# Filler matmuls in seven gaps of each of the first three tails of a decoder kernel

## The chip, the core and the metric

One core of a Trainium2 chip runs the whole kernel. TensorE (PE, matmuls), VectorE (DVE), ScalarE (ACT) and GpSimd (POOL) each work through an instruction list of their own in order and meet only at semaphores; SyncE (SP) issues most loads. PSUM has eight banks of 128 x 512 f32; matmuls write there. The metric is the device time of one execution in microseconds (us), the median of three runs.

## The reference, cut to what matters

Four sequences of 512 tokens with 512 features pass through two layers of mixers, each followed by a layer norm:

```
x = layernorm(x + mamba_A(x))        # selective scan over 1024 channels, then a gated MLP of width 1408
x = layernorm(x + mamba_B(ctx, x))   # selective scan over 512 channels, gated by x
x = layernorm(x + moe(x))            # top 2 of 8 experts of width 352, and a shared MLP
x = layernorm(x + segment_attn(x))   # attention within groups of 4 and a learned memory
x = layernorm(x + cross(x, ctx))     # x times softmax(q k')
x = layernorm(x + bias_router(x))    # top 8 of 64 learned biases
selective scan:  h = exp(dt * A) * h + dt * B * u ;  y = sum_n C_n * h_n      (16 states n)
```

## The kernel before, in words

All arithmetic is f32. The work on one sequence has three parts.

**Heads** (tasks `c_*`, `p_*`) project and convolve the inputs of the two scans. Nearly all of them are done before the first tail begins.

**Units**: the scans. There are twelve units q, three for each sequence (one of 512 channels for mamba B, two of 512 channels for mamba A), each with 16 states n. A unit opens with four matmuls `dt_mm` (PE L899), each evacuated by two ACT instructions (L1321, L1322) before the next may start, since all go through bank 5. When the fourth is evacuated, ACT runs a chain of exp and log (`dt_exp`, `dt_b`, L1340 to L1351), and then DVE runs three products of 2048 elements (`dt_c`, L1603, L1608, L1614). A state then is a scan on DVE (`sa`, L1622), a product with B (L1535, from bank 5) and one with C (`sb`, L1630, from bank 7); PE broadcasts the rows of B and C into these banks (L787, L916), ACT makes exp(dt * A) into `da` (L1169), POOL adds up y (L1895). `fin` (L1636) closes a unit.

**Tails**: all else of a sequence b, one long chain of small dependent stages. In order: `mix` (output projection, L942, eight tasks, with `x1` L1649 on DVE), `t_sq` and `t_rs` (sum of squares on PE L950, its root on ACT, the scaling on DVE L1655), the gated MLP (`ffn_mm`/`ffn_mu` L969/L976, `ffn_ev` L1661/L1667, `ffn_down` L777), `res_t` (L1028), layer norm `ln 0` (DVE L1484 to L1491, ACT L1160 to L1421), `v_in` (L1043), `gate` (ACT L1430, DVE L1706/L1709, PE L1059), `ln 1`, its transposes `ln_t 1` (L1035) with an evacuation on ACT (L1426), routing, the shared MLP (`exp_*`), 15 expert blocks (`bx`, `bg`, `bt`, `bd`), a gather by POOL, `comb` (DVE L1687), `ln 2`, segment attention (`s_in`, `seg_*`, L1778), `ln 3`, cross attention (`xmix`, L1127), `ln 4`, and the biases (`bias_*`, PE L1134 to L1149).

Tail b of the first three sequences runs on PE while DVE scans the three units of sequence b + 1. `mix` of tail b + 1 needs the last `fin` of these units and the last `xmix` of tail b. So from there on what is left of the old tail (`ln 4` and the biases), the opening of a unit and the new `mix` are interleaved; I call this stretch a handover. The last tail has no scans beside it.

**What sets the order**: `plan()` lists every task and engine with a rank, a duration in us and what it comes after; `schedule()` simulates these and picks, on the engine that can start first, the task of the lowest rank that can start within `SLACK` of it. The order that comes out is written into each engine's instruction list. So a task that is added, or that must come after another, can change the order on all engines. On the chip nothing is picked: a task waits for its turn and its semaphores.

`KEEP` lists 14 places in the last tail: after a task, before a task, a count. There PE multiplies a constant matrix by a constant into bank 7, which no one reads. `plan()` gives such a task 0.43 us a matmul and makes the task named second wait for it.

## Time and profile before

| | |
|---|---|
| runs | 3093.26 us median (3091.72 to 3096.84) |
| profiled execution | 3097.64 us, span 3095.8 us |
| PE busy | 2570.3 us (83%) |
| DVE busy | 2407.2 us (78%) |
| ACT busy | 1242.9 us (40%) |
| POOL busy | 1053.6 us (34%) |
| granted TensorE clock, mean | 0.893 |
| matmuls into bank 7 from constants (L1039) | 100, in the last tail alone |

The clock is a share of full speed, which is 2.4 GHz; the rows show 1.00 and 0.50 (1.2 GHz), and values between them where a stretch holds both. The profile shows each f32 matmul as two instructions. A row of the timeline has the start, the time that its instructions span, the engine and line, what is written from what, the number of instructions, and in brackets how long the engine had been idle before and what ended that.

### The profile page before, as it was taken

To read this page: it belongs to the slowest core of one execution; us is meant where nothing else is said; L and a number is where in the kernel's file an instruction comes from. 1 tells how busy PE (TensorE), PEld (TensorE's weight loads), DVE (VectorE), ACT (ScalarE), POOL (GpSimd) and SP (SyncE) were. 2 spreads that over 40 slices of the span, in tenths; PEclk is the share of its full clock that TensorE was granted. 3 is DMA by queue.
4 is the path that set the end of the run, shared out by engine and by line. 5 is a ranking of instruction groups with operands and counts; after the bars stand their busy time and mean duration, and the time that the engine had idled before them with its cause. 6 is when DMAs were issued, how large, how long until landed. Compare 5 with 4: busy or idle time off the path is not lost.

```text
span 3095.8 us, 21549 instructions
## 1 busy us (share of the span) xinstructions
PE 2570.3 (83%) x6908; PEld 1236.9 (40%) x6908; DVE 2407.2 (78%) x1788; ACT 1242.9 (40%) x1993; POOL 1053.6 (34%) x299
## 2 busy tenths in 40 slices
PE   4787989888969887699798785898787859999996
PEld 1234434333434443344344443343444424455553
DVE  4996898998979988989899999798999984121122
ACT  4433456444253453453534534534445332021222
POOL 1333343344434446424434454245343441000000
PEclk6886999888989998789889997899898869999998
DMA  3124435323212674032126660221166502216920
GB/s 132 36 82 153 137 104 189 110 92 109 64 39 72 220 236 153 25 101 63 41 72 202 219 182 13 89 82 48 65 198 189 173 27 75 72 48 221 293 86 14
DMA packets 160392, 350.15 MB, mean 113 GB/s; under 512 B 30680, under 2 KB 48088, under 8 KB 155608
## 3 DMA queue, kind: packets, MB, share of 16 engines
q1 hardware_dynamic: 134680, 271.89, 28.5%
q10 hardware_dynamic: 20480, 60.10, 5.1%
q0 software_dynamic: 5120, 16.78, 1.6%
q8 instruction: 55, 0.90, 0.1%
q14 instruction: 57, 0.47, 0.0%
HBM read 304.55 MB, written 61.73 MB: 118 GB/s over the span
## 4 chain that ended last, share of the span: by engine, by line
PE 39%; DVE 33%; issue 12%; ACT 8%; POOL 4%; DMA 3%; ACTq 0%; DVEq 0%; SPq 0%; POOLq 0%
DVE hb L1622 14%; PE ps L969 6%; PE ps L976 6%; DVE hb L1630 4%; DVE hb L1535 4%; PE ps L777 3%; PE ps L824 3%; POOL ya L1895 3%; PE ps L831 2%; PE ps L942 2%; DMA ring<-in_w_edn 2%; PE ps L1012 2%; PE ps L1127 2%; PE ps L899 1%; ACT T L1421 1%
## 5 line engine op out<-in xcount | busy, mean ns | idle before, releaser
L1895 POOL TENSOR_TENSOR ya<-ya,hb 128x2048 f32<-128x2048 f32 x188 | 856.8, 4557 | 1327.9 <-DVE hb L1622 1245.1
L1622 DVE TENSOR_TENSOR_SCAN hb<-da,hb 128x2048 f32<-128x2048 f32 x192 | 855.9, 4458 | 2.0 <-ACT da L1169 0.7
L1169 ACT ACTIVATE da<-dl,pk 128x511 f32<-128x511 f32 x768 | 489.3, 711 | 403.6 <-DVE hb L1622 393.3
L1535 DVE TENSOR_TENSOR hb<-du,ps 128x2048 f32<-128x2048 f32 x192 | 435.8, 2270 | 35.2 <-POOL ya L1895 27.4
L1630 DVE TENSOR_TENSOR hb<-hb,ps 128x2048 f32<-128x2048 f32 x192 | 437.4, 2278 | 3.7 <-PE ps L916 2.9
L824 PE MATMUL ps<-V,ring 128*128 128x512 f32 x512 | 245.1, 632 | 23.4 <-DVE V L1563 11.5
L777 PE MATMUL ps<-ring,hid 128*128 128x512 f32 x544 | 246.8, 610 | 3.7 <-DVE hid L1667 3.7
L993 PE MATMUL ps<-ring,hid 128*128 128x352 f32 x480 | 199.1, 498 | 22.4 <-ACT hid L1392 16.7
L997 PE MATMUL ps<-ring,hid 128*128 128x352 f32 x480 | 194.0, 487 | 11.5 <-ACT X L1409 11.4
L1012 PE MATMUL ps<-ring,X 128*128 128x512 f32 x360 | 180.9, 638 | 15.7 <-DMA ring<-in_w_edn 15.0
L969 PE MATMUL ps<-T,ring 128*128 128x512 f32 x352 | 165.7, 615 | 14.9 <-DVE T L1655 14.9
L787 PE MATMUL ps<-bct,sel 64*128 64x512 f32 x192 | 100.8, 525 | 88.1 <-DVE hb L1535 78.2
L824 PEld LDWEIGHTS ps<-V,ring 128*128 128x128 f32 x512 | 101.9, 203 | 157.5 <-issue 142.5
L976 PE MATMUL ps<-T,ring 128*128 128x512 f32 x352 | 159.5, 596 | 0.0
L777 PEld LDWEIGHTS ps<-ring,hid 128*128 128x128 f32 x544 | 104.0, 194 | 135.9 <-issue 135.9
L916 PE MATMUL ps<-bct,sel 64*128 64x512 f32 x192 | 91.3, 476 | 78.9 <-DVE hb L1630 78.8
L1160 ACT ACT_TABLE_LOAD x44 | 56.5, 1283 | 231.8 <-DVE mv L1491 188.8
L787 PEld LDWEIGHTS ps<-bct,sel 64*128 64x128 f32 x192 | 37.1, 193 | 222.2 <-DVE hb L1535 108.4
L997 PEld LDWEIGHTS ps<-ring,hid 128*128 128x128 f32 x480 | 94.7, 203 | 74.1 <-ACT X L1409 24.3
L942 PE MATMUL ps<-yg,ring 128*128 128x512 f32 x256 | 122.6, 636 | 0.7 <-DVE yg L1636 0.7
L1672 DVE SCALAR_TENSOR_TENSOR T<-T,ps 128x352 f32<-128x352 f32 x60 | 30.5, 508 | 116.5 <-ACT T L1397 116.5
L993 PEld LDWEIGHTS ps<-ring,hid 128*128 128x128 f32 x480 | 88.4, 201 | 77.1 <-issue 40.3
(285 smaller groups left out, 3511.8 us busy)
## 6 DMA issues: line engine op xcount, KB each, us to landing
ring<-egu SPq DMA_DIRECT2D x240, 352.0 KB, 3.8
ring<-in_w_edn SPq DMA_DIRECT2D x72, 512.0 KB, 5.3
ring<-in_w_fgu SPq DMA_DIRECT2D x44, 512.0 KB, 3.6
hid<-xrows SPq DMA_DIRECT2D x60, 256.0 KB, 4.4
yrows<-X ACTq DMA_DIRECT2D x60, 256.0 KB, 4.4
ring<-wc SPq DMA_DIRECT2D x24, 512.0 KB, 4.2
ring<-in_w_egu SPq DMA_DIRECT2D x24, 512.0 KB, 3.5
ring<-in_w_edn SPq DMA_DIRECT2D x60, 192.0 KB, 4.0
```

What stands on the lines that cost most here:

```text
L777: i = pe.matmul(ps[:, e, :], hid[:, k - lo, e * P:(e + 1) * P], cur["down"][:, base:base + HID], start=(k == lo and done == 0), stop=(k == ...
L824: i = pe.matmul(ps[:, bank(b, n), :], cur["w"][:, o:o + P], hx[:, k, :], start=(k == 0), stop=(k == KC - 1))
L969: i = pe.matmul(ps[:, b0, :], w[:, k * P:(k + 1) * P], src[:, k, :], start=(k == 0), stop=(k == KC - 1))
L976: i = pe.matmul(ps[:, 2 * (n % 2) + 1, :], cur["gu"][:, o:o + P], src[:, k, :], start=(k == 0), stop=(k == KC - 1))
L993: pe.matmul(ps[:, 2 * (j % 2), 0:FE], xt(j)[:, k * P:(k + 1) * P], w[:, 0:FE], start=(k == 0), stop=(k == KC - 1))
L997: pe.matmul(ps[:, 2 * (j % 2) + 1, 0:FE], xt(j)[:, k * P:(k + 1) * P], w[:, FE:2 * FE], start=(k == 0), stop=(k == KC - 1)).then_inc(s["bg ...
L1012: x = pe.matmul(ps[:, 2 * (j % 2) + 1, :], ht_(j)[0:rows, f:f + P], w[0:rows, o:o + HID], start=(i == 0), stop=(i == len(FB) - 1))
L1169: i = act.activation(dav(n % 2)[:, k, 1:], dl[:, k, 1:], ACT.Exp, scale=Aneg[:, (4 * (u % 3 - 1) if u % 3 else UC) + k, m:m + 1])
L1535: dve.tensor_tensor(hbv(m % NHB), du[:, :, :], wide(ps[:, 5, :], 4), ALU.mult).then_inc(s["dbu"], 1)
L1622: dve.tensor_tensor_scan(hb[:, h, :], da[:, b % 2, :], hb[:, h, :], 0.0, ALU.mult, ALU.add)\
L1630: dve.tensor_tensor(hbv(h), hbv(h), wide(ps[:, 7, :], 4), ALU.mult).then_inc(s["hc"], 1)
L1895: pool.tensor_tensor(sums, ya[:, :, :], hbv(m % NHB), ALU.add).then_inc(s["acc"], 1)
```

## The change

A second list, `KEEP_CYCLE`, names seven places for each of the first three tails, with 7, 4, 18, 4, 3, 6 and 12 matmuls (54 in a tail, 162 in all). They are of the same kind and size as those of the last tail (128 x 256), and write the upper half of bank 4. The first task of the next tail, `mix`, must come after the seventh group. Nothing else is edited.

```diff
+KEEP_CYCLE = [(("res_t", 0), ("v_in", 0), 7), (("gate", 0), ("ln_t", 1), 4), (("exp_down", 5), ("ln_t", 2), 18),
+              (("ln_t", 2), ("s_in", 0), 4), (("s_in", 1), ("seg_e", 0), 3), (("seg_t", 0), ("ln_t", 3), 6),
+              (("xmix", 3), ("ln_t", 4), 12)]
 ...
-    for i, ((t0, n0), (t1, n1), count) in enumerate(KEEP):
-        put(75, ("keep", SEQS - 1, i), "pe", 0.43 * count, ((t0, SEQS - 1, n0), "pe"))
-        nodes[(t1, SEQS - 1, n1), "pe"][2].append((("keep", SEQS - 1, i), "pe", 0))
+    for b in range(SEQS):
+        for i, ((t0, n0), (t1, n1), count) in enumerate(KEEP if b == SEQS - 1 else KEEP_CYCLE):
+            put(75, ("keep", b, i), "pe", 0.43 * count, ((t0, b, n0), "pe"))
+            nodes[(t1, b, n1), "pe"][2].append((("keep", b, i), "pe", 0))
+    for b in range(1, SEQS):
+        nodes[("mix", b, 0), "pe"][2].append((("keep", b - 1, len(KEEP_CYCLE) - 1), "pe", 0))
 ...
                     elif t == "keep":
-                        for _ in range(KEEP[n][2]):
-                            pe.matmul(ps[:, 7, 0:2 * P], ones, pk[:, 0:2 * P], start=True, stop=True)
+                        spare = ps[:, 7, 0:2 * P] if b == SEQS - 1 else ps[:, 4, 2 * P:4 * P]
+                        for _ in range((KEEP if b == SEQS - 1 else KEEP_CYCLE)[n][2]):
+                            pe.matmul(spare, ones, pk[:, 0:2 * P], start=True, stop=True)
```

Since the order is simulated, more moves than is added. Three places matter. In the changed kernel all lines below the list are three higher, those below the second edit six, and those below the third seven (L899 is L905, L942 is L948, L1127 is L1134, L1321 is L1328).

**PE at the handover from the first tail to the second** (L1127 is `xmix`, L899 `dt_mm`, L942 `mix`, L1035 `ln_t 4`, L1134 `bias_a`). Before:

```order
L916 MATMUL ps<-bct,sel 128x512
L899 MATMUL ps<-bcf,ring 128x512
L1127 MATMUL ps<-V,X 128x512 x4
L899 MATMUL ps<-bcf,ring 128x512
L1127 MATMUL ps<-V,X 128x512 x4
L899 MATMUL ps<-bcf,ring 128x512 x2
L787 MATMUL ps<-bct,sel 128x512
L942 MATMUL ps<-yg,ring 128x512 x16
L1035 MATMUL ps<-pk,T 128x128 x16
L942 MATMUL ps<-yg,ring 128x512 x4
```

Now:

```order
L922 MATMUL ps<-bct,sel 128x512
L905 MATMUL ps<-bcf,ring 128x512
L1134 MATMUL ps<-V,X 128x512 x4
L905 MATMUL ps<-bcf,ring 128x512
L1134 MATMUL ps<-V,X 128x512 x4
L905 MATMUL ps<-bcf,ring 128x512
L1046 MATMUL ps<-pk 128x256 x12
L905 MATMUL ps<-bcf,ring 128x512
L948 MATMUL ps<-yg,ring 128x512 x4
L1041 MATMUL ps<-pk,T 128x128 x16
L793 MATMUL ps<-bct,sel 128x512
L948 MATMUL ps<-yg,ring 128x512 x12
```

The seventh group (L1046) stands between the third and the fourth `dt_mm`, and the transposes of `ln 4` have moved ahead of the first row of B and of twelve of the `mix` matmuls.

**ACT at the same place** (L1321/L1322 evacuate a `dt_mm`, L1340 to L1351 are the exp and log chain, L1160 to L1421 are `ln 4`). Before, from the end of the fourth evacuation:

```order
L1322 ACTIVATE hb<-ps,pk 128x512
L1340 ACT_TABLE_LOAD
L1342 ACTIVATE hb<-hb 128x2048
L1348 ACT_TABLE_LOAD
L1349 ACTIVATE hb<-hb 128x2048
L1351 ACTIVATE da<-hb 128x2048
L1336 ACTIVATE ya<-yb,pk 128x512 x4
L1160 ACT_TABLE_LOAD
L1161 ACTIVATE sm<-mv,pk 128x4
L1163 ACTIVATE sm<-sm 128x4
L1417 ACTIVATE sm<-mv,sm 128x1 x4
L1421 ACTIVATE T<-ps,sm 128x512 x4
```

Now, from the end of the third:

```order
L1329 ACTIVATE hb<-ps,pk 128x512
L1167 ACT_TABLE_LOAD
L1168 ACTIVATE sm<-mv,pk 128x4
L1170 ACTIVATE sm<-sm 128x4
L1424 ACTIVATE sm<-mv,sm 128x1 x4
L1428 ACTIVATE T<-ps,sm 128x512 x4
L1328 ACTIVATE dl<-ps,pk 128x512
L1329 ACTIVATE hb<-ps,pk 128x512
L1347 ACT_TABLE_LOAD
L1349 ACTIVATE hb<-hb 128x2048
L1355 ACT_TABLE_LOAD
L1356 ACTIVATE hb<-hb 128x2048
```

The whole layer norm has moved from behind the chain of the new unit to ahead of its last evacuation. The second handover has the same move, and at the gate of the first tail `ln 0` makes it. At the gates of the second and third tails `ln 0` stood ahead of the third evacuation and now stands ahead of the second, the tanh of `gate` with it ahead of the third, and on ACT and DVE `ln 1` has moved ahead of the first factors (L1169) and products of the unit.

**PE at the end of the third tail**, where no unit opens (L1127 `xmix`, L942 `mix` of the last tail, L950 its `t_sq`). Before:

```order
L1127 MATMUL ps<-V,X 128x512 x16
L942 MATMUL ps<-yg,ring 128x512 x12
L1035 MATMUL ps<-pk,T 128x128 x16
L942 MATMUL ps<-yg,ring 128x512 x4
L1134 MATMUL ps<-pk,X 128x64 x16
L942 MATMUL ps<-yg,ring 128x512 x8
L1140 MATMUL ps<-pk,hid 64x128 x4
L942 MATMUL ps<-yg,ring 128x512 x4
L1149 MATMUL ps<-eb,hid 128x512 x4
L942 MATMUL ps<-yg,ring 128x512 x4
L950 MATMUL ps<-hid,pk 128x512 x4
```

Now:

```order
L1134 MATMUL ps<-V,X 128x512 x16
L1046 MATMUL ps<-pk 128x256 x12
L948 MATMUL ps<-yg,ring 128x512 x8
L1041 MATMUL ps<-pk,T 128x128 x16
L948 MATMUL ps<-yg,ring 128x512 x4
L1141 MATMUL ps<-pk,X 128x64 x16
L948 MATMUL ps<-yg,ring 128x512 x8
L1147 MATMUL ps<-pk,hid 64x128 x4
L948 MATMUL ps<-yg,ring 128x512 x4
L1156 MATMUL ps<-eb,hid 128x512 x4
L948 MATMUL ps<-yg,ring 128x512 x8
L956 MATMUL ps<-hid,pk 128x512 x4
```

Twelve filler matmuls stand between `xmix` and the first `mix`; the pieces of the old tail have moved ahead by one `mix` task each.

## Rows read from the trace of the kernel before

**Rows 1.** Busy times by stretch: second, third, last tail; last three columns: clock, DMA share, GB/s.

```profile
1315.00:1946.00 631.00, 517.24 (x1417) 252.21 (x1416) 574.47 (x409) 277.96 (x451) 259.62 (x71) 0.89 0.35 112
1946.00:2572.00 626.00, 509.20 (x1383) 250.25 (x1383) 567.16 (x384) 265.97 (x434) 260.02 (x71) 0.88 0.33 106
2572.00:3096.00 524.00, 476.04 (x1541) 259.78 (x1539) 114.15 (x278) 117.38 (x221) 19.84 (x17) 0.97 0.37 119
```

**Rows 2.** Waits of VectorE in the second tail, us in total, times, longest.

```profile
DVE hb L1603 <- ACT da L1351: 15.8, 2, 9.9
DVE hb L1535 <- POOL ya L1895: 9.1, 1, 9.1
```

**Rows 3.** Timeline of TensorE, last tail: twelve filler matmuls.

```profile
2735.83 5.34 PE L1039 MATMUL ps<-pk 128*128 128x256 f32 x24
```

**Rows 4.** Timeline at the gate of the first tail, ScalarE and VectorE.

```profile
892.88 0.68 ACT L1322 ACTIVATE hb<-ps,pk 128x512 f32<-128x512 f32 x1
...
891.89 0.17 DVE L1491 TENSOR_SCALAR mv<-mv 128x4 f32<-128x4 f32 x1
901.98 2.29 DVE L1603 SCALAR_TENSOR_TENSOR hb<-hb,da 128x2048 f32<-128x2048 f32 x1 [9.92 <-ACT da L1351]
...
911.99 0.69 DVE L1706 SCALAR_TENSOR_TENSOR T<-T 128x512 f32<-128x512 f32 x1 [3.07 <-ACT T L1430]
```

**Rows 5.** Timeline at the first handover, ScalarE and VectorE.

```profile
1310.90 0.68 ACT L1322 ACTIVATE hb<-ps,pk 128x512 f32<-128x512 f32 x1
...
1313.64 0.68 ACT L1322 ACTIVATE hb<-ps,pk 128x512 f32<-128x512 f32 x1
...
1325.18 1.28 ACT L1160 ACT_TABLE_LOAD   x1
...
1327.93 2.78 ACT L1421 ACTIVATE T<-ps,sm 128x512 f32<-128x512 f32 x4
...
1322.75 2.29 DVE L1603 SCALAR_TENSOR_TENSOR hb<-hb,da 128x2048 f32<-128x2048 f32 x1 [9.95 <-ACT da L1351]
```

**Rows 6.** Timeline at the end of this handover, TensorE and VectorE.

```profile
1357.91 5.01 PE L1149 MATMUL ps<-eb,hid 64*128 64x512 f32 x8 [1.45 <-DVE hid L1817]
1362.85 5.74 PE L950 MATMUL ps<-hid,pk 128*128 128x512 f32 x8
...
1373.14 2.74 DVE L1655 SCALAR_TENSOR_TENSOR T<-V,pk,R 128x512 f32<-128x512 f32 x4 [5.57 <-ACT sm L1163]
```

**Rows 7.** Timeline at the gate of the second tail, ScalarE and VectorE.

```profile
1527.02 0.68 ACT L1322 ACTIVATE hb<-ps,pk 128x512 f32<-128x512 f32 x1
...
1536.12 2.29 DVE L1603 SCALAR_TENSOR_TENSOR hb<-hb,da 128x2048 f32<-128x2048 f32 x1 [5.83 <-ACT da L1351]
...
1542.98 2.48 DVE L1484 BATCH_NORM_STATS2 sm<-ps 128x6 f32<-128x512 f32 x4
...
1550.60 4.42 DVE L1622 TENSOR_TENSOR_SCAN hb<-da,hb 128x2048 f32<-128x2048 f32 x1
...
1557.75 2.28 DVE L1535 TENSOR_TENSOR hb<-du,ps 128x2048 f32<-128x2048 f32 x1
1559.95 2.28 DVE L1630 TENSOR_TENSOR hb<-hb,ps 128x2048 f32<-128x2048 f32 x1
```

**Rows 8.** Longest wait of VectorE in the second tail's shared MLP, 1545 to 1620.

```profile
DVE hid L1667 <- PE ps L976: 2.2, 1, 2.2
```

**Rows 9.** Timeline at the end of the third tail, VectorE and TensorE.

```profile
2523.29 1.12 DVE L1778 SCALAR_TENSOR_TENSOR hid<-ps,sm,pk 128x128 f32<-128x128 f32 x4 [1.76 <-PE ps L1108]
...
2572.40 10.46 PE L942 MATMUL ps<-yg,ring 128*128 128x512 f32 x24
...
2610.40 3.70 PE L950 MATMUL ps<-hid,pk 128*128 128x512 f32 x8 [0.78 <-DVE V L1649]
```

**Rows 10.** Timeline of TensorE: transposes of `ln 3` and of `ln 4`, first tail.

```profile
1284.42 3.68 PE L1035 MATMUL ps<-pk,T 128*128 128x128 f32 x16 [7.37 <-ACT T L1421]
...
1330.95 1.92 PE L1035 MATMUL ps<-pk,T 128*128 128x128 f32 x16
```

## The prediction
> **What bounds the kernel now.** I read the busy times by stretch first [rows 1]. In the second and third tails VectorE works 574 of 631 us and 567 of 626: it is the bound, with 57 and 59 us of idle time each, and TensorE has 114 and 117 us. In the last tail VectorE works 114 of 524 us and the chain through TensorE is the bound. The clock is 0.88 to 0.89 in the cycles and 0.97 in the last tail, where fillers run today. So a filler can help in the first three tails only where VectorE waits, in the end, for a matmul that ran at half clock. The waits of VectorE come next [rows 2]: in the second tail 15.8 us are for the exp and log chain on ScalarE that opens a unit, up to 9.9 at a time, and 9.1 are for GpSimd, which is issuing the gather. Neither is a wait for a slow matmul. Then I walked the timeline at the places where the order of instructions changes.
>
> **What is added.** Twelve fillers at full clock took 5.34 us in the last tail, 0.43 to 0.44 each [rows 3]. The 54 of a tail are 23.5 us at full clock, 70 us in three tails, against more than 340 us in which TensorE idles there. The first six groups lie in waits for ScalarE or VectorE. An example is the gap before the transposes of `ln 3`, 7.37 us [rows 10], which takes six fillers of 2.6 us. I cost these six at nothing in themselves. Without that cover each would cost its own length, 1.3 to 7.8 us. What costs is the new order, and the seventh group.
>
> **Gate of the first tail: +2.2.** Before, ScalarE evacuated the fourth `dt_mm` at 892.88 to 893.56 and opened the unit's chain at once [rows 4]. Now `ln 0` stands ahead of it. Its statistics are there at 892.06 [rows 4]; on ScalarE a layer norm takes 5.5 us, from 1325.18 to 1330.71 in the handover [rows 5]; the evacuation takes some 1.3 more (two instructions of 0.68). That ends at 898.9, 5.3 late. The three products of VectorE then start at 907.3 instead of 901.98 and end at 914.2, where the gating before began at 911.99 after a wait of 3.07 [rows 4]. So the wait goes, and 914.2 - 912.0 = 2.2 us stay. Bounds: 0 and 5.3.
>
> **The two handovers: +1.2 each.** The third evacuation ends at 1311.58 [rows 5]. With `ln 4` (5.5) and the fourth (1.3) behind it the chain begins at 1318.4 and not at 1314.32: 4.1 late, and so is the product at 1322.75 on which VectorE had waited 9.95 us already [rows 5]. TensorE's twelve fillers lie within that delay. What counts is when the scaling for the next MLP can start (1373.14, after a wait of 5.57 for the root [rows 6]). In the new order VectorE has the bias softmax ahead of a scan and the last `x1` behind it (4.42 [rows 7]), so that `t_sq` can only start some 4 us later than it did. Before, it ran slow, 5.74 us behind 5.01 for the bias product [rows 6], against 3.70 for the same `t_sq` at full clock [rows 9]. If the `mix` matmuls that now stand between these pieces keep the clock up, the root comes 0.6 us earlier than before; if not, 2.9 later. I take the middle, 1.2, twice: 2.4.
>
> **Gates of the second and third tails: +1.0 each.** Two evacuations now follow the tanh where one did. A round of `dt_mm` and evacuation is 2.7 us (1310.90 to 1313.64 [rows 5]), so the product at 1536.12 [rows 7] comes at 1538.8. In exchange the statistics of `ln 1` (2.48 and two small ones, 3.0 [rows 7]) are done within the wait ahead of it. But ScalarE now does `ln 1` before the unit's first factors: 1541.3 + 5.5 + 2.5 = 1549.4 at the earliest for the first scan, which was at 1550.60 with 2.3 us of convolution ahead of it that now come after it. 1549.4 + 2.3 - 1550.6 is 1.1; the same for the third tail gives 1.0. Bounds: -0.3 (the statistics cover all) and 2.7. Together 2.0.
>
> **Third tail: -1.8.** `comb` and `ln 2` now stand one scan earlier, so the wait of 1.76 for the segment scores [rows 9] should go. Bounds: -1.8 and 0.
>
> **Transposes of `ln 3`: -1.5 in all.** They took 3.68 us at half clock after the idle time, those of `ln 4` took 1.92 at full clock [rows 10], so 1.76 can be saved in each tail. Two things stand against it: between the fillers and these transposes some 4.6 us of idle time stay, in which the clock may fall all the same, and the next row of C has to wait for VectorE anyway. I take 0.5 each; bounds 0 and 1.76. The Trainium skill ("TensorE: Matmul & The Clock Gate", Part 4, PE-mode transpose) says that the full clock does not engage for transposes. By it this term would be 0 and the sum 1.5 higher; the trace disagrees, since sixteen transposes took 1.92 against 3.68 us.
>
> **End of the third tail: +5.2.** No unit opens here. TensorE works from 2572.40 to 2610.40 without a pause but 0.78 us [rows 9], first at `mix`; VectorE and ScalarE wait for it. The twelve fillers stand right ahead of the first `mix`, the clock is full, and nothing covers them: 12 x 0.43 = 5.2. The 0.78 could give a little back, but in the new order the last `mix` is the last thing ahead of `t_sq`. Bounds: 4.4 and 5.3. This is the term I trust most, since it needs no story about the clock.
>
> **Sum.** 2.2 + 2.4 + 2.0 - 1.8 - 1.5 + 5.2 = 8.5. The profiled execution took 3097.64 us, which gives 3106; it lay 4.4 above the median, so I predict 3093.3 + 8.5 = 3102. The shared MLP and the expert blocks are reordered too, in the second tail most; there I take 0, with -2.2 a tail (the longest wait in the MLP [rows 8]) and +9.0 (one state, 4.42 + 2.28 + 2.28 [rows 7]) as the ends.
>
> **Rivals.**
>
> *A. The full clock pays (3084).* Both transposes of each tail that run slow (`ln 2`, `ln 3`) save their 1.76 us in full and VectorE feels all of it, 10.6 us; the handovers end 0.6 early; the MLPs lose their wait of 2.2 in two tails: 2.2 - 1.2 + 2.0 - 1.8 - 10.6 - 4.4 + 4.4 = -9.4. For it speaks that the clock is 0.88 here and 0.97 where fillers run [rows 1]. Against it: VectorE is busy while the transposes of `ln 2` run, and the order does not let it take the tail's work earlier. The Trainium skill ("TensorE: Matmul & The Clock Gate", Why this matters for your kernels) advises to leave no idle gaps between bursts of matmuls, or the clock goes back to half; by that rule alone this change is right.
>
> *B. No change (3094).* An earlier `ln 1` lets the shared MLP start some 5 us earlier at the second and third gates, and VectorE's waits there go; the handovers end 0.6 early: 2.2 - 1.2 + 2.0 - 1.8 - 1.5 - 4.4 + 5.2 = 0.5. For it: the new order starts this work earlier relative to the scans. Against it: these waits are short [rows 8].
>
> *C. The blocks come late in the second tail (3109).* There four convolution tasks of the next sequence now stand between the fourth and the fifth chunk of the shared MLP, each needing VectorE between scans. TensorE then reaches the expert blocks one state later and must be done with them by the same state as before. Up to 9.0 us can become a wait of VectorE or GpSimd; with 114 us of idle time TensorE regains some. I add 6.8. It decides as soon as the blocks' rate, not VectorE, sets the pace.
>
> *D. The fillers do not hold the clock (3107).* The handovers cost 2.9 each and the transposes save nothing: 2.2 + 5.8 + 2.0 - 1.8 + 5.2 = 13.4. The change then only occupies TensorE. The idle time left ahead of the transposes speaks for it.
>
> **How the numbers follow.** Forecast 0.33 (its own range 3097 to 3107), A 0.15, B 0.25, C 0.15, D 0.12. A difference of 0.2%, 6.2 us, is about what a measurement of this kernel can tell from none: faster is below 3087.1, slower above 3099.4. A alone is faster; B and a small part of the forecast are the same; the rest is slower: 0.15, 0.28, 0.57. The range from 3089 to 3111 leaves out most of A and the far ends of C and D.
>
> **What the profile after would show.** The end of the third tail: 24 filler instructions of some 5.2 us ahead of the first `mix`, and from there to the end the same times as before. The wait of VectorE for the chain that opens a unit: longer by 5 at the first gate (15 instead of 9.9), by 4 at the handovers. The wait of 3.07 for the tanh in the first tail gone. `t_sq` in the handovers at 3.7 us or at 5.7. Transposes of `ln 3` at 1.9 or at 3.7. The prediction is wrong if VectorE's idle time in the second and third tails falls below 57 and 59 us, or if the start of the last tail's `mix` is less than 5 us later than before.

## The result, and the profile after

The changed kernel takes 3095.85 us (median of 20 runs, 3090.67 to 3108.24), the kernel before 3091.6 (20 runs). The ratio is 1.0018, with a 95% interval of 1.0009 to 1.0026: 3 to 8 us slower, where 8.5 was forecast, and within what a measurement of this kernel can hardly tell from none. The traced execution has a span of 3091.5 us. One of the twelve executions of experiment 12, 4375.91 us at a clock of 0.55, is in its median below but not in its ratio.

Busy time by stretch of the changed kernel (columns as in [rows 1]):

```profile
1315.00:1946.00 631.00, 540.74 (x1544) 272.75 (x1543) 567.09 (x409) 279.95 (x453) 266.34 (x72) 0.92 0.34 112
1946.00:2572.00 626.00, 522.91 (x1467) 269.06 (x1466) 566.85 (x390) 261.30 (x431) 261.19 (x71) 0.89 0.33 107
2572.00:3092.00 520.00, 473.59 (x1537) 260.29 (x1535) 115.19 (x272) 112.57 (x211) 20.08 (x17) 0.97 0.37 118
```

TensorE is busier by 14 to 24 us a cycle, and the clock rose by 0.03 in the second tail and by 0.01 in the third, against [rows 1]. VectorE still has 59 to 64 us of idle time in each.

The heads, which no kernel here touches, took from 6.6 us less to 3.0 us more than in the execution shown of before. So two executions are compared by marks, each counted from the first `mix` of its own trace. Behind it two executions of one kernel (experiments 9 and 12) agree within 0.1 us at the marks up to the last tail's `mix`, and so do 3 and the changed kernel, which differ only later. One pair does not: experiment 7 and the changed kernel run the same lists up to the gate of the third tail and lie 4.0 us apart there. So a stretch of one traced execution can be off by as much as 4 us. The marks are the first `xmix` of a tail, the scaling of the next MLP (`t_rs`, L1655) and the first `mix` of the last tail. The last tail itself varied from 520.3 to 524.2 us over all kernels.

| stretch, between marks | before | forecast | changed | its order without fillers |
|---|---|---|---|---|
| first tail, `t_rs` to `xmix` | 544.1 | +1.7 | +0.8 | +4.5 |
| first handover, `xmix` to `t_rs` | 80.7 | +1.2 | -5.1 | -5.2 |
| second tail | 550.4 | +0.5 | +1.4 | +1.1 |
| second handover | 80.8 | +1.2 | -5.1 | -5.3 |
| third tail | 554.4 | -1.3 | +7.0 | +7.1 |
| `xmix` to the last `mix` | 13.7 | +5.2 | +5.2 | 0.0 |
| sum | | +8.5 | +4.1 | +2.3 |

The sums are those of the unrounded entries. The forecast column groups the terms on record by stretch, the transposes with their tails. The sum of the marks, 4.1, is what the medians show, 4.25. Two terms were wrong by more than the whole result, with opposite signs.

The first handover of the changed kernel, VectorE and ScalarE (answers [rows 5] and [rows 6]):

```profile
1305.86 0.68 ACT L1329 ACTIVATE hb<-ps,pk 128x512 f32<-128x512 f32 x1
1306.56 1.28 ACT L1167 ACT_TABLE_LOAD   x1
...
1312.53 0.71 ACT L1329 ACTIVATE hb<-ps,pk 128x512 f32<-128x512 f32 x1
1313.26 1.28 ACT L1347 ACT_TABLE_LOAD   x1
```

```profile
1342.58 0.42 DVE L1812 TENSOR_TENSOR hid<-hid,sm 128x256 f32<-128x256 f32 x1
...
1345.22 0.68 DVE L1656 TENSOR_TENSOR V<-ps,V 128x512 f32<-128x512 f32 x1
1345.82 4.41 DVE L1629 TENSOR_TENSOR_SCAN hb<-da,hb 128x2048 f32<-128x2048 f32 x1
...
1350.73 0.67 DVE L1656 TENSOR_TENSOR V<-ps,V 128x512 f32<-128x512 f32 x1
...
1363.00 2.74 DVE L1662 SCALAR_TENSOR_TENSOR T<-V,pk,R 128x512 f32<-128x512 f32 x4 [1.89 <-ACT sm L1170]
```

The same place on TensorE, with the end of the third tail behind the line of dots:

```profile
1305.17 5.45 PE L1046 MATMUL ps<-pk 128*128 128x256 f32 x24
...
1350.86 3.70 PE L1156 MATMUL ps<-eb,hid 64*128 64x512 f32 x8 [0.81 <-DVE hid L1824]
1354.49 3.70 PE L956 MATMUL ps<-hid,pk 128*128 128x512 f32 x8
...
2551.81 13.90 PE L1134 MATMUL ps<-V,X 128*128 128x512 f32 x32
2565.55 5.34 PE L1046 MATMUL ps<-pk 128*128 128x256 f32 x24
2570.73 7.03 PE L948 MATMUL ps<-yg,ring 128*128 128x512 f32 x16
```

The chain of the unit begins at 1313.26, 6.7 us behind the end of the third evacuation instead of 2.7 [rows 5], so the expected delay is there. But `t_sq` starts at 1354.49, which is 1360.3 with the 5.8 us of the heads, 2.6 us ahead of before; it takes 3.70 us where it took 5.74, and the wait for the root is 1.89 where it was 5.57 [rows 6]. The bias product ahead of it takes 3.70 us where it took 5.01. The granted clock of the whole handover is 0.99, and was 0.87. At the end of the third tail the twelve fillers lie bare ahead of `mix`.

What else stood in that place before is seen in two rows of the kernel before that the prediction did not read: VectorE's bias-softmax product, and GpSimd.

```profile
1349.39 4.38 DVE L1805 TENSOR_TENSOR hid<-hid,sm 128x256 f32<-128x256 f32 x1
```

```profile
1348.97 4.52 POOL L1895 TENSOR_TENSOR ya<-ya,hb 128x2048 f32<-128x2048 f32 x1 [23.76 <-DVE hb L1622]
```

The product took 4.38 us beside GpSimd's running sum and ended 0.3 us behind it; in the changed kernel GpSimd is idle at 1342.58 and it takes 0.42. The Trainium skill ("SBUF — State Buffer", SBUF: two separate sides) says that VectorE and GpSimd share one port pair, which is an exclusive lock held for the whole instruction, and that a VectorE operation with two inputs in SBUF is blocked by a GpSimd operation that reads SBUF. By that rule, the trace agrees, in both kernels.

### The profile page after: what moved, and what is told of

It is laid out like the page before. It is cut to its first block, busy times and chain, and to the rows that moved or that the text cites. A ratio compares the mean times of both kernels' runs of the same rounds, so it can differ in the third digit from the quotient of the medians.

```text
span 3091.5 us, 22199 instructions
## 1 busy us (share of the span) xinstructions
PE 2618.4 (85%) x7232; PEld 1294.3 (42%) x7232; DVE 2400.7 (78%) x1788; ACT 1241.6 (40%) x1993; POOL 1061.8 (34%) x299
## 4 chain that ended last, share of the span: by engine, by line
PE 40%; DVE 32%; issue 12%; ACT 8%; POOL 4%; DMA 3%; ACTq 0%; DVEq 0%; SPq 0%; POOLq 0%
DVE hb L1629 13%; PE ps L975 6%; PE ps L982 6%; DVE hb L1637 4%; PE ps L783 4%; DVE hb L1542 4%; PE ps L830 3%; POOL ya L1902 3%; PE ps L837 2%; PE ps L1018 2%; DMA ring<-in_w_edn 2%; PE ps L1134 2%; PE ps L948 1%; PE ps L905 1%; ACT T L1428 1%
## 5 line engine op out<-in xcount | busy, mean ns | idle before, releaser
L999 PE MATMUL ps<-ring,hid 128*128 128x352 f32 x480 | 193.2, 485 | 14.5 <-ACT hid L1399 9.0
L1003 PE MATMUL ps<-ring,hid 128*128 128x352 f32 x480 | 189.7, 478 | 14.2 <-ACT X L1416 14.0
L1018 PE MATMUL ps<-ring,X 128*128 128x512 f32 x360 | 188.3, 658 | 9.1 <-DMA ring<-in_w_edn 7.4
L783 PEld LDWEIGHTS ps<-ring,hid 128*128 128x128 f32 x544 | 104.1, 194 | 135.4 <-issue 135.4
L1046 PE MATMUL ps<-pk 128*128 128x256 f32 x524 | 130.4, 405 | 0.0
L1003 PEld LDWEIGHTS ps<-ring,hid 128*128 128x128 f32 x480 | 92.3, 197 | 74.2 <-ACT X L1416 27.1
L793 PEld LDWEIGHTS ps<-bct,sel 64*128 64x128 f32 x192 | 36.9, 192 | 195.9 <-issue 95.1
L948 PE MATMUL ps<-yg,ring 128*128 128x512 f32 x256 | 116.4, 607 | 0.7 <-DVE yg L1643 0.7
```

The lines of the kernel that those rows point to most:

```text
L783: i = pe.matmul(ps[:, e, :], hid[:, k - lo, e * P:(e + 1) * P], cur["down"][:, base:base + HID], start=(k == lo and done == 0), stop=(k == ...
L999: pe.matmul(ps[:, 2 * (j % 2), 0:FE], xt(j)[:, k * P:(k + 1) * P], w[:, 0:FE], start=(k == 0), stop=(k == KC - 1))
L1003: pe.matmul(ps[:, 2 * (j % 2) + 1, 0:FE], xt(j)[:, k * P:(k + 1) * P], w[:, FE:2 * FE], start=(k == 0), stop=(k == KC - 1)).then_inc(s["bg ...
L1018: x = pe.matmul(ps[:, 2 * (j % 2) + 1, :], ht_(j)[0:rows, f:f + P], w[0:rows, o:o + HID], start=(i == 0), stop=(i == len(FB) - 1))
```

## The experiments

Each run was compared with the kernel before on the same chip. "Mark" is how much later the last tail's `mix` starts than before, counted from the first `mix`, in the one traced execution of each kernel. It is free of the heads and of the last tail, but not of the chance of up to 4 us that experiment 7 shows. The medians of the kernel before were 3092.7 to 3094.1 us on these chips.

| kernel | mark, us | median | ratio (95%) |
|---|---|---|---|
| changed | +4.1 | 3095.85 | 1.0018 (1.0009 to 1.0026) |
| 1 its order, no fillers | +2.3 | 3095.29 | 1.0003 (0.999 to 1.0016) |
| 2 its fillers, old order | +21.1 | 3111.85 | 1.0068 (1.0049 to 1.0087) |
| 3 last seventh group silent | -0.9 | 3089.57 | 0.9989 (0.9976 to 1.0003) |
| 4 GpSimd's sum waits | 0.0 | 3092.12 | 1.0002 (0.999 to 1.0014) |
| 5 handover groups alone | -4.3 | 3087.54 | 0.9979 (0.9968 to 0.999) |
| 6 the same, silent | -3.5 | 3093.22 | 0.9988 (0.9974 to 1.0003) |
| 7 first two tails alone | -4.1 | 3089.64 | 0.998 (0.9965 to 0.9994) |
| 8 norm early, no more | +6.8 | 3099.92 | 1.002 (1.0009 to 1.0031) |
| 9 without the first two groups | -6.6 | 3081.46 | 0.996 (0.9945 to 0.9974) |
| 10 order of the first group | +16.1 | 3109.71 | 1.005 (1.0033 to 1.0068) |
| 11 first group, third tail | +5.9 | 3098.03 | 1.0015 (1.0003 to 1.0027) |
| 12 as 9, again | -6.7 | 3083.84 | 0.9971 (0.9959 to 0.9982) |

### 1. The new order without its fillers

```diff
-                        for _ in range((KEEP if b == SEQS - 1 else KEEP_CYCLE)[n][2]):
+                        for _ in range(KEEP[n][2] if b == SEQS - 1 else 0):
```

> Same instruction order as the changed kernel on every engine, but the 162 filler matmuls of the first three tails are not issued. Theory O (the new order gives the gain at the two handovers, the fillers only occupy TensorE): the bias-softmax product stays at 0.42 us instead of 4.38 in both handovers, the start of the last tail's mix comes 5.2 us earlier than in the changed kernel, and the whole takes about 3090.5 us, ratio to the kernel before 0.9995. Theory C (the fillers' full clock gives it): the product is short, but t_sq and the bias product run at half clock again (5.7 and 5.0 us instead of 3.7), each handover loses some 2 to 3 us against the changed kernel, and the whole is 3094 to 3096, ratio 1.001.

Order it is, at the handovers: without a single filler both are as short as with them (the table above), the product takes 0.42 us, and `t_sq` and the bias product take 3.70 us each. So the full clock there does not need the fillers, and theory C falls. The last `mix` comes only 1.9 us earlier than in the changed kernel, though, and not 5.2, since theory C holds at another place: the end of the first tail. TensorE in this run, and then in the changed kernel:

```profile
1249.56 3.78 PE L1057 MATMUL ps<-T,pk 128*128 128x512 f32 x4 [1.18 <-ACT X L1433]
...
1265.03 4.54 PE L1128 MATMUL ps<-pseg,hid 128*128 128x512 f32 x6 [0.69 <-ACT hid L1467]
...
1280.97 3.68 PE L1041 MATMUL ps<-pk,T 128*128 128x128 f32 x16 [8.08 <-ACT T L1428]
...
1285.72 5.54 PE L1061 MATMUL ps<-T,pk 128*128 128x512 f32 x8
```

```profile
1249.58 1.99 PE L1057 MATMUL ps<-T,pk 128*128 128x512 f32 x4 [1.18 <-ACT X L1433]
...
1263.81 2.84 PE L1128 MATMUL ps<-pseg,hid 128*128 128x512 f32 x6 [0.69 <-ACT hid L1467]
...
1279.74 3.40 PE L1041 MATMUL ps<-pk,T 128*128 128x128 f32 x16 [8.07 <-ACT T L1428]
...
1283.83 3.70 PE L1061 MATMUL ps<-T,pk 128*128 128x512 f32 x8
```

Both traces have the same offset of the heads, so the rows compare directly. With fillers three pieces run at full clock, and `xmix` starts 3.7 us earlier. That gain is kept to the end of the third tail (3.3), where the seventh group takes 5.2. The transposes (L1041) stay slow behind 8 us of idle time.

### 2. The fillers in the old order

Planned as before; then, into TensorE's finished list:

```diff
+    for b in range(SEQS - 1):
+        for i, ((t0, n0), (t1, n1), _) in enumerate(KEEP_CYCLE):
+            at = order["pe"].index((t0, b, n0)) + 1 if i == 6 else order["pe"].index((t1, b, n1))
+            order["pe"].insert(at, ("keep", b, i))
```

> The order of the kernel before on every engine, with the same seven groups of fillers put into TensorE's list by hand (six directly ahead of the task that they precede, the seventh directly behind the last xmix). Theory O: the bias-softmax product takes 4.4 us in both handovers as before; nothing is gained there; the seventh group costs 5.2 at the end of the third tail: about 3097 us, ratio 1.0018 (up to 1.003 if the seventh group is on the path at the handovers too). Theory C: the handovers gain 2 to 4 us each from full clock (t_sq 3.7 instead of 5.74), and the whole is 3090 to 3093, ratio 1.000.

Far worse than either theory: 21.1 by the mark. In the old order the twelve of the seventh group lie bare ahead of `mix` at every handover. From `xmix` to `mix` it takes 4.9 to 5.2 us longer all three times. Another 3.5 us are lost in the second tail, which alone would be within the 4 us of chance, and 6.1 in the third. So the seventh group is free only where the plan has made room for it, and the first six, which I costed at nothing, cost nothing in the new order; in the old one they may not be free.

### 3. The seventh group of the third tail, silent

```diff
+                        if b == SEQS - 2 and n == 6:
+                            continue
```

> The changed kernel in its own order, only the twelve fillers of the seventh group in the third tail are not issued. If the twelve lie bare on the path to the last tail: 5.2 us less than the changed kernel, about 3090.6, ratio to the kernel before 0.9997. If the last tail takes back what they cost, or the clock falls without them: 3094 to 3096, ratio 1.001.

The mark comes 5.1 us earlier than in the changed kernel, and the marks ahead of it are the same within 0.1. The fillers lie bare there, as predicted.

### 4. GpSimd's sum waits for the product

```diff
+                        if b in (6 * NST, 9 * NST):
+                            pool.wait_ge(*of("ft", u // 3 - 2 + u % 3, 6))
```

> The kernel before, in which GpSimd's sum of the first state of the second and of the third cycle also waits until VectorE has made the bias-softmax product (about 1 us later than it starts now). Theory P (an instruction of VectorE with two operands in SBUF that starts beside a running sum of GpSimd stands until that sum ends): the product takes 0.42 instead of 4.38 us twice, each handover ends up to 4 us earlier, the whole is 3 to 8 us faster: 3084 to 3088, ratio 0.998. Rival Q (the long product is only a symptom, what follows it waits for TensorE or for the sum anyway): the product is short, but x1, t_sq and the root come at the same time as before: 3091 to 3092, ratio 1.000. Rival R (the long duration has another cause than GpSimd): the product stays at 4.4 us.

VectorE in this run, first handover:

```profile
1346.21 0.42 DVE L1805 TENSOR_TENSOR hid<-hid,sm 128x256 f32<-128x256 f32 x1
...
1348.21 3.39 DVE L1812 TENSOR_TENSOR hid<-hid 128x256 f32<-128x256 f32 x1
```

Theory P is right about the cause and wrong about the gain. The product takes 0.42 us, and the next one with two operands in SBUF, 0.42 long before, stands for 3.39 until the sum (now 1346.81 to 1351.32) ends. The collision only moved to the next candidate. The first handover is 0.4 us shorter. The second is 3.9 us shorter, but there `t_sq` took 3.70 us instead of 6.04, and at the next gate the gain was gone. Removing one blocked instruction is not the handover's gain.

### 5 and 6. The seventh group of the first two tails alone, and silent

```diff
+            if b == SEQS - 2 or b < SEQS - 2 and i != 6:
+                continue
```

and for 6 also the edit of experiment 1. In both, the last seventh group's edge to `mix` is gone too. Of the whole new order only the two handovers are left.

> Only the seventh group of the first and of the second tail, and the order that the planner makes of it: it differs from the kernel before at the two handovers and nowhere else. Theory K (each handover is 5.0 us shorter by its order, and nothing takes that back when the rest of the tails keeps the old order): 10 us less than the kernel before, 3081 to 3084, ratio 0.9967. Theory G (the time gained is given back before the next tail, because VectorE then stands in the old waits of the tail and in other blocked instructions): 3088 to 3092, ratio 0.9995.

> The same order as the run with the seventh group of two tails only, but its 24 filler matmuls are not issued. If only the order counts: the same time as with them, within 2 us. If the clock at the handover counts: 2 to 4 us a handover more. If the twelve lie partly on the path: some us less.

Between the theories. The first handover gains 5.1 us again, and 1.3 of it are given back by the next gate; the second gains 2.5, of which 0.4 is left at the next gate, and the mark ends 4.3 ahead. VectorE waits there for TensorE, whose `mix` matmuls fell to half clock in the middle: eight took 6.58 us.

```profile
1968.94 6.58 PE L950 MATMUL ps<-yg,ring 128*128 128x512 f32 x8
```

```profile
1979.43 0.69 DVE L1658 TENSOR_TENSOR V<-ps,V 128x512 f32<-128x512 f32 x1 [2.46 <-PE ps L950]
```

Silent, the first handover gains only 2.7 us and the mark is 3.5 ahead. Now it is there that eight `mix` matmuls run at half clock:

```profile
1350.66 6.45 PE L950 MATMUL ps<-yg,ring 128*128 128x512 f32 x8
```

At the second handover it is the other way round: the silent run gains 5.3 us and the one with fillers 2.5. Over both handovers they gain 8.0 and 7.6. So at the handovers neither run shows that fillers earn anything. What they show is that a handover in the new order lasts 75.5 to 75.6 us when its middle `mix` matmuls keep the full clock and 78.0 or 78.2 when they lose it.

### 7. All groups in the first two tails, none in the third

```diff
+            if b == SEQS - 2:
+                continue
```

> All seven groups in the first and the second tail, none in the third, whose order is that of the kernel before from the second handover on. Theory T (the order of the third tail's middle costs 7.1 and its seventh group 5.1; the rest is as in the changed kernel): 12.2 less than the changed kernel and 8 less than the kernel before, 3083 to 3086, ratio 0.9974. Rival: the middle of the third tail takes back what the handover gained whatever its order: 5 less than the changed kernel, about 3091, ratio 0.9998.

The third tail in its old order takes the 554.4 us of before and nothing of the 7.0. But the mark is -4.1 and not -8: `xmix` of the second tail comes at +1.0 here, at -3.0 in the changed kernel. Up to the third tail the two kernels issue the same instructions in the same order, and their marks agree within 0.2 us until the first expert block; the 4 us arise behind it. The traces show where: at two places the same matmuls ran at full clock in the changed kernel and at half clock here. One is an opening of a unit, where VectorE then waits 5.61 us for the exp and log chain and in the changed kernel not at all (`comb` comes 1.4 us later); the other is the first step of the cross attention, behind the transposes of `ln 3`. The changed kernel, then this run:

```profile
1721.71 1.88 PE L1018 MATMUL ps<-ring,X 128*128 128x512 f32 x4
...
1911.24 3.70 PE L1061 MATMUL ps<-T,pk 128*128 128x512 f32 x8
```

```profile
1723.12 3.62 PE L1020 MATMUL ps<-ring,X 128*128 128x512 f32 x4
...
1913.30 6.02 PE L1063 MATMUL ps<-T,pk 128*128 128x512 f32 x8
```

Why the clock fell in one execution and not in the other is open.

### 8. Only the early norm

The finished lists of the kernel before, with `ln 4` on ScalarE ahead of the last evacuation, its transposes evacuated behind `skip`, and on TensorE behind the first `mix` (the head of the loop that moves them):

```diff
+    for e, task, spot in [("act", "ln", "dt_mm"), ("act", "ln_t", "skip"), ("pe", "ln_t", "mix"), ("pe", "dt_c", "ln_t")]:
```

> The kernel before with one part of the new order at both handovers: ScalarE does ln 4 ahead of the last evacuation and evacuates its transposes right behind the skip products, TensorE transposes behind the first mix; the bias router's steps, the scans, x1 and the later mix tasks keep their old places, and there are no fillers. If the early norm alone gives the gain: 5 us a handover, 3082 to 3085, ratio 0.997. If the gain comes from the bias steps and x1 standing ahead of a scan: nothing gained, or up to 4 us a handover lost for the later chain of the unit: 3092 to 3099, ratio 1.000 to 1.0025.

The mark is 6.8 us later: 3.0 at the first handover, -0.3 at the second, where `t_sq` took 3.70 us instead of 6.04, and 3.7 in the third tail. VectorE's wait at the first handover, against 9.95 in [rows 5]:

```profile
1329.45 2.29 DVE L1610 SCALAR_TENSOR_TENSOR hb<-hb,da 128x2048 f32<-128x2048 f32 x1 [13.93 <-ACT da L1358]
```

My 4.1 us for the later chain are real. The gain must then come from the rest of the order, bias steps and `x1` ahead of a scan among it, and from the clock of `t_sq`; no run takes that rest by itself.

### 9 and 12. Without the first two groups

```diff
+            if b < SEQS - 1 and i < 2 or b == SEQS - 2 and i == 6:
+                continue
```

> The third to the seventh group in the first two tails and the third to the sixth in the third tail; the first and second group, and the seventh of the third tail, are left out. The order of instructions is exactly that of the run with the seventh group of two tails only; what is added are the 31 fillers of groups three to six in each of three tails. Theory O (order alone counts): the time of that run, 3085 to 3089, ratio 0.998. Theory C (a fuller clock shortens these tails by the 3.8 us by which fillers shortened the end of the first tail in the changed kernel's order): 4 to 8 us less than that, 3079 to 3084, ratio 0.996. Rival W (the fillers stand in the way of the chain, as they did in the old order with all seven groups): 3 to 10 us more, 3090 to 3098.

> The kernel of the run without the first two groups once more, since that one had only five timed runs and its median lay 12 us below the kernel before while its marks lay 6.6 us ahead. If the marks are right: 3086 to 3088, ratio 0.998, and the rest was chance. If the fillers also bring something that the one traced execution does not show: 3081 to 3083 again, ratio 0.996.

The edge to the last `mix` is gone as in 5. The instruction order is that of experiment 5, and 93 more fillers are issued. The mark is -6.6 and -6.7. Both runs measured faster than the kernel before, by 13 and 9 us of median, with intervals that overlap (0.9959 to 0.9974). This is the best version. The medians show more than the marks in both runs; what lies behind that is open, and part may be the last tail (521.1 and 521.6 us, 523.4 before). Where experiment 5 had its slow `mix`, the second handover's `t_rs` now comes at -7.2 instead of -6.0:

```profile
1981.95 0.60 PE L1149 MATMUL ps<-pk,hid 128*64 128x128 f32 x4
1982.39 3.60 PE L950 MATMUL ps<-yg,ring 128*128 128x512 f32 x8
1986.79 3.70 PE L1158 MATMUL ps<-eb,hid 64*128 64x512 f32 x8 [0.80 <-DVE hid L1826]
1990.41 3.70 PE L958 MATMUL ps<-hid,pk 128*128 128x512 f32 x8
```

### 10 and 11. The first group alone

Of `KEEP_CYCLE` only the group ahead of `v_in`. Experiment 10 takes its order in three tails and issues none of its fillers; experiment 11 takes it in the third tail alone, seven fillers issued. The groups' edges to `mix` are gone in both. For 10, besides the edit of experiment 1:

```diff
+            if b < SEQS - 1 and i != 0:
+                continue
```

> Only the order that the planner makes of the first group (ahead of v_in) in each of the first three tails; its 21 filler matmuls are not issued, and the other six groups are not there. The handovers keep the old order. Theory F (this one group makes everything of the new order that costs: 4.5 us in the first tail, 1.2 in the second, 7.2 in the third, as the run with the whole new order and no fillers showed between its marks): 13 us slower than the kernel before, 3104 to 3107, ratio 1.004. Rival: most of that cost belongs to the handover's new order, which hands its gain back; then this order alone is 0 to 4 us slower, ratio 1.0005.

> Only the first group of the third tail, seven fillers, and the order that comes with it from the gate of the third tail on. Up to that gate nothing differs from the kernel before. Theory F: the last tail's mix starts 7 us later, 3100 us, ratio 1.0023. Rival (the cost only appears when the handover before was shorter): the last tail's mix starts within 2 us of before, ratio 1.000.

Theory F stands. The order of this one group costs 16.1 us in three tails, and 5.9 in the third alone, of the 7.0 there. By stretch experiment 10 does not split as theory F has it: the tails cost 4.5, 5.9 and 10.8 us where 4.5, 1.2 and 7.2 were expected, and the two handovers give 3.1 and 2.0 back. Planned by itself, of the six groups ahead of the handover only this one moves any instruction of the second and third tails. Experiment 11 repeats the pattern of the changed kernel's third tail: `route_a` 4.2 earlier, the first expert block 4.2 later, `xmix` 5.9 later. One piece of it, in the changed kernel, VectorE and then GpSimd:

```profile
2212.64 8.65 DVE L1629 TENSOR_TENSOR_SCAN hb<-da,hb 128x2048 f32<-128x2048 f32 x1
...
2515.70 3.43 DVE L1792 TENSOR_TENSOR hid<-hid 128x512 f32<-128x512 f32 x1
```

```profile
2201.82 4.31 POOL L1873 DMA_INDIRECT xrows<-T,hid  x1 [0.30 <-issue]
...
2212.48 4.52 POOL L1902 TENSOR_TENSOR ya<-ya,hb 128x2048 f32<-128x2048 f32 x1
...
2514.06 4.51 POOL L1902 TENSOR_TENSOR ya<-ya,hb 128x2048 f32<-128x2048 f32 x1 [4.42 <-DVE hb L1629]
```

The indirect DMAs of the scatter now stand one sum earlier in GpSimd's list, and its next sum starts 0.16 us ahead of a scan that reads two operands in SBUF. The scan takes 8.65 us instead of 4.42. In experiment 11 the same scan takes 8.03. But the kernel before had a blocked instruction of its own in this tail, which takes 2.29 us in the changed one, so by itself the blocked scan is no net loss of this tail:

```profile
2361.57 6.60 DVE L1636 SCALAR_TENSOR_TENSOR yg<-ya,yg 128x2048 f32<-128x2048 f32 x1 [6.97 <-POOL ya L1895]
```

The other row above is a product of the segment softmax, 1.56 us before and 3.43 now, under another sum.

The handovers of experiment 10 have the old order on every engine, no filler, and the product still takes 4.38 us. Yet the first one is 3.1 us shorter than before, with `t_sq` and the bias product at full clock:

```profile
1357.94 3.67 PE L1156 MATMUL ps<-eb,hid 64*128 64x512 f32 x8 [1.36 <-ACT T L1474]
1361.54 3.70 PE L956 MATMUL ps<-hid,pk 128*128 128x512 f32 x8
```

## Why the prediction came out as it did

**Slower, and by less than forecast.** The time fell inside the range, and the ratio's interval is above 1. The 4.1 us are not the forecast's sum made smaller: only some of its terms hold, and the errors of the others, -12.6 us at the two handovers and +8.3 in the third tail, nearly cancel. That the time fell inside the range is in good part luck. One of the prediction's own signs of being wrong did appear: the last `mix` starts 4.1 us later, less than the 5 that it had set. The other did not: by stretch VectorE idles 64 and 59 us, not less than 57 and 59.

**Gate of the first tail, +2.2: right.** The mark of the gating is +2.1, by the steps given: `ln 0` ahead of the fourth evacuation, the chain later, the wait for the tanh gone. In the changed kernel:

```profile
901.40 2.29 DVE L1610 SCALAR_TENSOR_TENSOR hb<-hb,da 128x2048 f32<-128x2048 f32 x1 [15.13 <-ACT da L1358]
...
908.26 0.68 DVE L1713 SCALAR_TENSOR_TENSOR T<-T 128x512 f32<-128x512 f32 x1
```

The wait is 15.13 where 9.92 was [rows 4], the 15 that was named, and the gating has no wait.

**End of the third tail, +5.2: right**, 5.2 by the marks and 5.1 in experiment 3. The 0.78 ahead of `t_sq` stayed.

**The handovers, +1.2 each: wrong in sign, -5.1 each.** The step that failed is "`t_sq` can only start some 4 us later than it did". I had carried the 4.1 us of ScalarE's chain through the whole handover. The delay of the chain is real (experiment 8), but it does not reach `t_sq`: counted from `xmix`, `t_sq` starts at 67.1 us instead of 70.4, 3.3 earlier. Counted over the handover, VectorE has the same three scans, 1.7 us less idle time (19.4 against 21.1) and none of the 4.0 us for which the product was blocked. That product was an ordinary row of 4.38 us of an instruction that needs 0.42, and I had not compared it with its neighbours. The lower bound of -0.6 a handover rested on the same step. Nor do the two bounds follow from the numbers beside them: 4.1 less 1.3 for the bias product and 2.0 for `t_sq` is +0.8, not -0.6.

The other half of that term, the clock, came true at its good end, without the fillers (experiment 1): of the 5.1 us at the first handover, 1.3 lie in the bias product and 2.0 in `t_sq`. But the clock alone does not give the gain, and the order alone does not either. From `xmix` to the gating of the next tail the new order was 3.6 to 4.7 us ahead of before in the fourteen handovers of all runs in which its middle `mix` matmuls kept the full clock, and 0.7 and 0.4 in the two in which they lost it (the first of experiment 6, the second of 5). The old order with `t_sq` at full clock was 0.2 ahead at the one handover that shows it cleanly (the second of experiment 4). What makes the clock hold or fall there is open; the fillers do not decide it.

**Gate of the second tail, +1.0, and its middle: near enough, in part by luck**, +1.4 for the tail where 0.5 was forecast; at the gate itself 0.7. With the same lists this tail was +5.3 in experiment 7. (The sum on record, 1541.3 + 5.5 + 2.5, is 1549.3 and not 1549.4; nothing hangs on it.) The convolution tasks in its shared MLP did delay the blocks, by 11.8 us from `route_a` to the first of them, as rival C said. But 7.2 came back before `comb` and 2.9 had been won ahead of `route_a`: TensorE had the room.

**Third tail, -1.3 with its gate, its scores and its transposes: wrong, +7.0.** The term that was mis-sized is the one I set to nothing, the reordered MLP and blocks, whose upper end of +9.0 was worked out and given to the second tail by rival C. From `route_a` to the first expert block this tail lost 9.1 us, and 2.5 of them came back by `comb`. The wait of 1.76 for the segment scores did go. But `comb` one scan earlier only put one more scan behind it: three stand between it and the scores where two stood. Over the tail VectorE has 46 scans in both kernels, 3.8 us more idle time (40.7 against 36.9) and 1.8 us more in blocked instructions. The rest of the 7.0, 1.4 us, I cannot assign.

**Transposes of `ln 3`, -0.5 each: not there.** They took 3.40 to 3.67 us, behind 5.5 to 8.1 us of idle time that the fillers did not cover. Those of `ln 2`, 0.7 to 1.5 us behind eighteen fillers, took 2.77 to 2.78 instead of 3.67 to 3.68, 0.9 less in each tail. In the first tail the fillers did shorten other pieces, worth 3.7 us, which is their only clear gain here. The Trainium skill ("TensorE: Matmul & The Clock Gate", Part 4) has transposes without the full clock, but the sixteen of `ln 4` took 1.91 us again; those of the changed kernel's first three tails that took 3.40 us or more all stand behind 5.5 to 8.8 us of idle time.

**Of the rivals**, B had a total close to the truth by another way than it gave: the MLP's waits did not pay, and the handovers gave 5.1 us each, not 0.6. D was right for the transposes and wrong for the handovers, where `t_sq` ran at full clock.

## What to carry to other kernels

A filler that a planner places is first an edit to the order of every engine: plan each group alone, see which one moves anything, and time the order without the fillers; here one group of seven matmuls carried most of the cost in the third tail and another all of the gain at the handovers. Before forecasting a handover, compare each row there with the shortest of its kind: a 4.38 beside a 0.42 is slack that a reordering may release. A filler is free only in a gap that the order leaves; the same fillers in the old order cost 21 us. And before a few us of one trace are given to an edit, look for matmuls of one form at two speeds: the same lists came out 4 us apart where such matmuls differed.

## What was not expected of the hardware

VectorE and GpSimd hold each other up for a whole instruction, in both directions. A product of 0.42 us took 4.38 and 3.39, and a scan of 4.42 took 8.65, each held until GpSimd's sum of 4.5 us had ended; and one of GpSimd's eight indirect DMA issues, 0.96 us each, took 4.31 beside a scan that had started 0.87 us earlier (2200.95, 4.42 long). Moving the sum by 1 us moved the collision to the next instruction with two operands in SBUF.

Fillers can run at half clock themselves. The eighteen ahead of `ln 2` in the first tail took 10.01 us where eighteen at the 0.445 of [rows 3] are 8.0:

```profile
1230.92 10.01 PE L1046 MATMUL ps<-pk 128*128 128x256 f32 x36
```
